# Shared and routed experts of a mixture layer as one sequence of 48 chunks

## Chip, cores, metric

One core of one Trainium2 chip. The time is the device time of one execution, in microseconds (us); of several runs the median counts. The kernel is an attention layer followed by a mixture-of-experts layer; the change touches the second.

## The reference

```python
# x: (8, 1024, 256) float32, after the attention layer; h = layernorm(x)
cap = 128                                  # int(1024 * 2.0 / 16)
scores = softmax(h @ gate_w.T).transpose(0, 2, 1)          # (8, 16, 1024)
topk_w, topk_idx = top_k(scores, cap)      # each expert takes 128 rows of each b
x_tok = take_along_axis(h[:, None], topk_idx[..., None], axis=2)
g = einsum('becd,efd->becf', x_tok, Wg)    # 16 experts, F = 512, D = 256
u = einsum('becd,efd->becf', x_tok, Wu)
eo = einsum('becf,edf->becd', gelu(g) * u, Wd) * topk_w[..., None]
flat = zeros((8 * 1024, 256)).at[flat_idx].add(eo)         # routed experts
shared = (gelu(h @ Ws_g.T) * (h @ Ws_u.T)) @ Ws_d.T        # shared expert, all rows
out = x + flat + shared
```

## The kernel before

The attention block comes first. It leaves in memory `out` (the layer's x), `xn2` (the normalised rows) and `xn2T` (the same, turned), and in SBUF `gate_scores`.

Then `feed_forward` (L931) runs twice, each time as a block of its own, at whose end all engines meet. The first call (`shared=True`) is the shared expert over all 8192 rows, in 16 chunks of 512 tokens. It also makes the lists: the 128 pairs of a row group b and an expert lie on 128 partitions, each with its 1024 scores, and 16 rounds on VectorE take the eight largest (`select`, parts 0, 1 and 2: maximum, index of the maximum, replacement by -1). The second call is the routed part: 16 experts with 8 x 128 gathered rows each, two chunks of 512 an expert, 32 chunks.

Matmuls are done in three passes for precision (`three`, L61 to L63): each operand is split into a high part (cast to fp32r, ScalarE) and a low part (the difference, VectorE). One chunk is, on TensorE, four groups `up` (each the gate and the up product for 128 of the 512 columns F, 12 matmuls of 512 columns) and one `down` (48 matmuls of 256 columns); the down product belongs to the chunk before and stands between group 1 and group 2. In the routed part the tokens of the next chunk are turned by eight transposes ahead of it (`turn_tokens`, L1377). In the shared part the tokens come turned out of `xn2T`.

The other engines' work for a chunk: ScalarE does four GELUs (L1194), four casts `high` (L1198), the cast of the next chunk's tokens (L1187 or L1190); VectorE four products (L1261), four `low` (L1265), the low part of the next tokens (L1253), the result of the chunk before (L1281 in the shared part, four scalings L1286 in the routed one), and in the shared part one round of selection. The results of the shared part are stored by SyncE, with x added; those of the routed part are added into `out` by GpSimd's indirect DMAs (`scatter`, L1152), four a chunk, as the gathers (`gather`, L1130) are. Weights of the next expert are split inside the chunks; two sets of split weights take turns, the shared expert uses set 1.

The order is that of the program on each engine. TensorE's `up(n, f)` waits for the product of the group two before (the banks `gu` are two), `down` for all four low parts of its chunk, a chunk's start for the low part of its tokens. All loops go through `groups`: a first body, a hardware loop over the middle ones, and a last body. In the shared call a body is two chunks (one b), in the routed one four (two experts).

At the end of the first call VectorE ends the lists, TensorE turns them (L1443, L1444), VectorE copies them to `taken_scores` and `taken_rows` (L1365, L1366). GpSimd does nothing in the first call; in the second it starts with the gathers of the routed chunks 0 and 1.

## Time and profile before

| | us |
|---|---|
| median of 3 runs | 2351.36 |
| the three runs | 2350.05 to 2356.03 |
| the profiled execution's own time | 2354.57 |
| its span, first to last instruction | 2352.2 |
| busy, share of the span: TensorE | 2186.0, 93% |
| VectorE | 1848.3, 79% |
| ScalarE | 1557.9, 66% |
| GpSimd | 1051.3, 45% |

The profile's page gives busy time by engine, then the span in 40 slices of 58.8 us with the clock that TensorE was granted. The attention block takes slices 1 to 25, the shared part runs from about 1480 to 1755 us, the routed part from about 1757 to the end. In the page's slices TensorE's digit is 9 nearly throughout, and 7 in the slice in which the shared part ends. A matmul's duration in the profile is longer than its distance to the next one, since matmuls are pipelined; what a piece of work costs TensorE is read from start to start.

### The profile page before, as it was taken

The page shows a single profiled execution, that of the slowest core. Times are in us where ns is not written, and L with a number is a line of the kernel's source. Part 1 is how long each engine was busy: PE and PEld are TensorE (multiplying, and loading weights), DVE is VectorE, ACT ScalarE, POOL GpSimd, SP SyncE. Part 2 cuts the span into 40 slices and gives each one's busy share as a digit, 9 for nine tenths or more (in the row PEclk, how much of TensorE's full clock was granted, in tenths as well). Part 3 has the DMA queues.
Part 4 walks back from the last instruction along what each step waited for, and adds up shares of the span by engine and source line. Part 5 has one row for each costly group of instructions (what it writes and reads, how often), then busy time and mean ns, then how long its engine had stood idle before and what let it go on. Part 6 is the DMA issues. An engine that isn't in the chain of part 4 may idle for free. (4 is left out here: it accounts for less than half of the span.)

```text
span 2352.2 us, 42150 instructions
## 1 busy us (share of the span) xinstructions
PE 2186.0 (93%) x15502; PEld 1270.0 (54%) x15502; DVE 1848.3 (79%) x3103; ACT 1557.9 (66%) x3056; POOL 1051.3 (45%) x1561
## 2 busy tenths in 40 slices
PE   4899999999999999999999997899979999999996
PEld 3233333334333333343333224788868888888986
DVE  4899999999999999999999993566654555555553
ACT  2489999999998998998998895333323334334332
POOL 4442555564465456456451220000004666666664
PEclk8699999999999999999999998899999999999998
DMA  4002013112122122122122012432313444544543
GB/s 114 5 26 35 17 41 71 35 45 67 35 67 65 33 61 53 35 61 51 35 59 46 24 44 74 135 107 81 106 61 101 105 101 107 109 96 109 112 91 36
DMA packets 204835, 156.19 MB, mean 66 GB/s; under 512 B 110080, under 2 KB 185728, under 8 KB 204672
## 3 DMA queue, kind: packets, MB, share of 16 engines
q1 hardware_dynamic: 180096, 120.47, 18.3%
q0 software_dynamic: 24576, 33.57, 8.3%
q8 instruction: 100, 1.64, 0.3%
q14 instruction: 63, 0.52, 0.1%
HBM read 78.50 MB, written 50.33 MB: 55 GB/s over the span
## 5 line engine op out<-in xcount | busy, mean ns | idle before, releaser
L604 DVE TENSOR_REDUCE sb_MX<-ring 128x1 f32<-128x512 f32 x2048 | 1281.7, 683 | 65.6 <-PE ring L874 41.9
L718 ACT ACTIVATE sb_PR<-rot 128x512 f32<-128x512 f32 x2048 | 1118.3, 610 | 124.0 <-PE rot L885 108.7
L874 PE MATMUL ring<-sb_KT,sb_QT 32*128 32x512 bf16 x2048 | 503.7, 391 | 76.4 <-DVE sb_MX L604 63.0
L896 PE MATMUL pv<-sb_PR,sb_VA 128*32 128x512 f32 x4096 | 548.0, 607 | 2.6 <-ACT sb_OT L770 0.6
L874 PEld LDWEIGHTS ring<-sb_KT,sb_QT 32*128 32x128 bf16 x2048 | 122.0, 91 | 674.1 <-DVE sb_MX L604 620.6
L885 PE MATMUL rot<-sb_QT,sb_KT 32*128 32x512 bf16 x2048 | 405.7, 386 | 0.9
L1194 ACT ACTIVATE ex_GL<-ex_gu 128x512 f32<-128x512 f32 x128 | 76.5, 598 | 348.6 <-PE ex_gu L63 346.4
L1261 DVE TENSOR_TENSOR ex_HF<-ex_GL,ex_gu 128x512 f32<-128x512 f32 x128 | 87.5, 683 | 252.1 <-ACT ex_GL L1194 252.1
L1109 POOL TENSOR_TENSOR ex_pool_scratch<-identity 128x1 f32<-128x1 f32 x96 | 35.4, 369 | 461.4 <-POOLq L951 316.6
L1152 POOL DMA_INDIRECT out<-ex_YS,ex_rows_out x128 | 209.9, 1640 | 43.6 <-issue 43.1
L61 PE MATMUL ex_gu<-ex_XH,weights_high 128*128 128x512 f32 x512 | 201.0, 393 | 2.4 <-DVE ex_XL L1253 2.4
L62 PE MATMUL ex_gu<-ex_XL,weights_high 128*128 128x512 f32 x512 | 200.6, 392 | 0.0
L63 PE MATMUL ex_gu<-ex_XH,weights_low 128*128 128x512 f32 x512 | 200.3, 391 | 0.0
L61 PE MATMUL ex_y<-weights_high,ex_HH 128*128 128x256 f32 x512 | 147.4, 288 | 2.9 <-DVE ex_HL L1265 2.9
L896 PEld LDWEIGHTS pv<-sb_PR,sb_VA 128*32 128x32 f32 x4096 | 80.7, 108 | 123.6 <-issue 67.3
L1194 ACT ACTIVATE sh_GL<-sh_gu 128x512 f32<-128x512 f32 x64 | 38.2, 597 | 162.8 <-PE sh_gu L63 162.8
L62 PE MATMUL ex_y<-weights_low,ex_HH 128*128 128x256 f32 x512 | 144.8, 283 | 0.0
L63 PE MATMUL ex_y<-weights_high,ex_HL 128*128 128x256 f32 x512 | 144.8, 283 | 0.0
L1130 POOL DMA_INDIRECT ex_XG<-xn,ex_rows_in x128 | 126.0, 984 | 39.7 <-issue 39.1
L61 PE MATMUL rot<-sb_WH,sb_XH 128*128 128x256 f32 x384 | 129.8, 338 | 15.0 <-ACT sb_PR L718 6.0
L388 POOL CAST sb_QP<-sb_MX 128x16 bf16<-128x16 f32 x64 | 16.3, 254 | 242.8 <-DVE sb_MX L610 242.7
L1261 DVE TENSOR_TENSOR sh_HF<-sh_GL,sh_gu 128x512 f32<-128x512 f32 x64 | 43.7, 683 | 91.7 <-ACT sh_GL L1194 91.7
(170 smaller groups left out, 4108.3 us busy)
## 6 DMA issues: line engine op xcount, KB each, us to landing
sb_XA<-x SPq DMA_DIRECT2D x8, 1024.0 KB, 5.4
sb_XR<-x SPq DMA_DIRECT2D x8, 1024.0 KB, 5.3
out<-sb_XR SPq DMA_DIRECT2D x8, 1024.0 KB, 4.5
xn<-sb_XN SPq DMA_DIRECT2D x8, 1024.0 KB, 4.6
xn2T<-sb_XT SPq DMA_DIRECT2D x8, 1024.0 KB, 4.2
sh_XG<-xn2T SPq DMA_DIRECT2D x16, 512.0 KB, 5.4
sh_X<-out SPq DMA_DIRECT2D x16, 512.0 KB, 4.8
weights<-WgT SPq DMA_DIRECT2D x16, 512.0 KB, 4.2
```

The costliest lines, as they stand in the source:

```text
L61: nc.tensor.matmul(out, a_hi, b_hi, start=first, stop=False)
L62: nc.tensor.matmul(out, a_hi, b_lo, start=False, stop=False)
L63: return nc.tensor.matmul(out, a_lo, b_hi, start=False, stop=last)
L604: nc.vector.reduce_max(MX[:, unit % 2, half, j, qt % 4:qt % 4 + 1], ring[m % RING][:], AX.X).then_inc(ring_done, 1)
L718: out = nc.scalar.activation(PR[V % P_STEPS][:, j, :], R[:], ACT.Exp, scale=0.25)
L874: nc.tensor.matmul(ring[m % RING][:], QT[g][r, P * qt:P * qt + P], KT[g][r, 512 * half:512 * half + 512], start=True, stop=True, tile_posi ...
L885: nc.tensor.matmul(R[:], KT[g][r, P * kt:P * kt + P], QT[g][r, 512 * qh:512 * qh + 512], start=True, stop=True, tile_position=(r.start, 0) ...
L896: out = nc.tensor.matmul(pv_bank[head(j), :], VA[b % 2][:, kt, 4 * g + j, :], PR[V % P_STEPS][:, j, :], start=(kt == 0), stop=(kt == TT - 1))
L1130: nc.gpsimd.indirect_dma_start(out=XG[k % 2][:, t, :], out_offset=None, in_=d["xn2"], in_offset=bass.IndirectOffsetOnAxis(ap=rows_in[:, b: ...
L1152: nc.gpsimd.indirect_dma_start(out=d["out"], out_offset=bass.IndirectOffsetOnAxis(ap=rows_out[:, b:b + 1], axis=0), in_=YS[k % 2][:, t, :] ...
L1194: nc.scalar.activation(GL[f % 2][:], gu[f % 2][:, 0, 0:N], ACT.Gelu).then_inc(gelu_ready, 1)
L1261: nc.vector.tensor_tensor(HF[f % 2][:], GL[f % 2][:], gu[f % 2][:, 1, 0:N], ALU.mult).then_inc(hf_ready, 1)
```

## The change

The two calls become one block with one sequence of 48 chunks: 16 shared (0 to 15) and 32 routed (16 to 47). `Chunk` holds what differs between them, `following` and `before` give the neighbours, so that the last shared chunk turns the tokens of the first routed one and the first routed chunk holds the down product and the result of the last shared one. `turn_tokens`, the splits and the waits count through. The tiles of the two calls become one set; the turned shared tokens lie in the same buffers `XG` as the gathered ones, as a view `XT`.

The selection gets its own place: four groups of two chunks with three rounds (5 and 4 parts), then two groups with two rounds (3 and 3 parts), then none in the last four chunks. In a chunk up to two parts stand behind the first two products and `low` 0, the others at the chunk's end. The result of the chunk before, which stood behind `product` 2 and `low` 1, now stands ahead of `product` 2, in all chunks. The lists are finished behind chunk 11, turned ahead of chunk 14 and copied there; GpSimd's gathers wait for `lists_ready` only. The weights of expert 0 are split inside chunks 14 and 15. SyncE stores the last shared chunk, then loads the weights of expert 1.

The core of the diff (blank lines left out):

```diff
-def feed_forward(nc, d, ident, SC, WT, IX, W, WH, WL, shared_out, B, shared):
+def feed_forward(nc, d, ident, SC, B):
...
+    SHARED = RS * KS
     ROUNDS = CAP // 8
-    SHARED_STORES = 16 * B * HALVES // 2
-    tag = "sh_" if shared else "ex_"
+    THREES, TWOS = 4, 2
+    STORED = 16 * RS
+    ROWS = 16 * CT
...
+        XT = [x[:].rearrange("p t d -> p (t d)").rearrange("p (k n) -> p k n", k=KD) for x in XG]
...
+        def groups(engine, body, R, upto=None, since=0):
+            upto = R if upto is None else upto
+            if since == 0:
+                body(0, True, False)
+                since = 1
+            if min(upto, R - 1) > since:
+                with engine.Fori(since, min(upto, R - 1)) as r:
                     body(r, False, False)
-            if R > 1:
+            if upto == R:
...
+                self.n = KS * r + k if shared else SHARED + KE * r + k
+                self.nth = r if shared else 2 * r + k // 2
+                self.expert = None if shared else 2 * r + k // 2
+                self.q = 1 if shared else k // 2 % 2
+                self.turn = 0 if shared else self.expert + 1
+                self.x_in = shared_in[self.c] if shared else gathered[self.c]
+                self.x_count = (16 if shared else 16 * CT) * (self.nth + 1)
+                self.ys_before = self.n if shared else SHARED + CT * (self.n - SHARED)
...
+            groups(sp, shared_group, RS)
+            store(RS - 1, KS - 1)
+            def load_next(e):
+                sp.wait_ge(wl_ready, 3 * (turn_of(e) + 1))
+                load_weights(e + 1)
+            for c in range(2):
+                sp.wait_ge(gathered[c], ROWS)
+            load_next(0)
+            with sp.Fori(1, E - 1) as e:
+                load_next(e)
...
+                if known(ch.n, SHARED + 2):
+                    pool.wait_ge(xl_ready, ch.n - 1)
+                else:
+                    pool.wait_ge(turned_full, ch.n - SHARED - 1)
...
+            pool.wait_ge(lists_ready, 1)
             own = Tally(settled)
-            gather(0, 0, own)
-            gather(0, 1, own)
+            gather(Chunk(False, 0, 0), own)
+            gather(Chunk(False, 0, 1), own)
...
+            groups(act, lambda r, first, last: [chunk(Chunk(True, r, k), last) for k in range(KS)], RS)
+            groups(act, lambda r, first, last: [chunk(Chunk(False, r, k), last) for k in range(KE)], RE)
...
+            def chunk(ch, first, last, own=None, s=0, parts=range(0)):
+                def choose(n, more=False):
+                    for p in parts[n:] if more else parts[n:n + 1]:
+                        select(s + p // 3, p % 3, own)
+                after = following(ch, last)
+                past = before(ch, first)
+                coming = coming_expert(ch, last)
+                product(ch, 0)
+                product(ch, 1)
+                low(ch, 0)
+                choose(0)
+                choose(1)
+                if after:
+                    split_tokens(after)
+                if past:
+                    result(past)
+                product(ch, 2)
+                low(ch, 1)
+                product(ch, 3)
+                low(ch, 2)
+                if coming:
+                    split_weights(*coming, 0 if ch.k % 2 == 0 else 2)
+                if coming and ch.k % 2 == 1:
+                    take_scores(*coming)
+                low(ch, 3)
+                if coming and ch.k % 2 == 0:
+                    split_weights(*coming, 1)
+                choose(2, True)
+            split_weights(None, 1, 0)
+            split_weights(None, 1, 1)
+            split_tokens(Chunk(True, 0, 0))
+            split_weights(None, 1, 2)
+            dve.wait_ge(sct_full, 1)
+            nc.vector.tensor_copy(sct[:], y[0:BE].rearrange("p a n -> p (a n)")).then_inc(sct_ready, 1)
+            dve.wait_ge(sct_ready, 1)
+            def three_rounds(r, first, last):
+                own = Tally(own_sem, 9 * r)
+                chunk(Chunk(True, r, 0), first, last, own, 3 * r, range(0, 5))
+                chunk(Chunk(True, r, 1), False, last, own, 3 * r, range(5, 9))
+            def two_rounds(r, first, last):
+                s = 3 * THREES + 2 * (r - THREES)
+                own = Tally(own_sem, 3 * s)
+                chunk(Chunk(True, r, 0), False, last, own, s, range(0, 3))
+                chunk(Chunk(True, r, 1), False, last, own, s, range(3, 6))
...
+            assert 3 * THREES + 2 * TWOS == ROUNDS
+            groups(dve, three_rounds, RS, THREES)
+            groups(dve, two_rounds, RS, THREES + TWOS, THREES)
+            own = Tally(own_sem, 3 * ROUNDS)
+            own.wait(dve)
+            own.inc(nc.vector.tensor_copy(indf[:], inds[:]))
+            own.wait(dve)
+            dve.wait_ge(row0_in, 16)
+            nc.vector.tensor_scalar(indf[:], indf[:], row0[:], None, ALU.add).then_inc(sel_ready, 1)
+            groups(dve, shared_group, RS, RS - 1, THREES + TWOS)
+            dve.wait_ge(sel_full, 1)
+            own.inc(nc.vector.tensor_copy(taken_scores[:].rearrange("p b e -> p (b e)"), turned[:, 0, 0:BE]))
+            nc.vector.tensor_copy(taken_rows[:].rearrange("p b e -> p (b e)"), turned[:, 1, 0:BE]).then_inc(lists_ready, 1)
+            own.wait(dve)
+            shared_group(RS - 1, False, True)
+            groups(dve, group, RE)
+            result(Chunk(False, RE - 1, KE - 1))
...
-                    product(n, 0)
-                    product(n, 1)
-                    low(n, k, 0)
-                    if shared:
-                        select(TURNS * n, 0, own)
-                    if not final:
-                        split_tokens(r if k < K - 1 else r + 1, (k + 1) % K)
-                    product(n, 2)
-                    low(n, k, 1)
-                    if shared:
-                        select(TURNS * n, 1, own)
-                    if not (first and k == 0):
-                        result(r if k else r - 1, (k - 1) % K)
-                    product(n, 3)
-                    low(n, k, 2)
-                    if more:
-                        split_weights(e, q, 0 if k % HALVES == 0 else 2)
-                    if more and k % HALVES == 1:
-                        take_scores(e, q)
-                    low(n, k, 3)
-                    if more and k % HALVES == 0:
-                        split_weights(e, q, 1)
-                    if shared:
-                        select(TURNS * n, 2, own)
-                        for s in range(1, TURNS):
-                            for part in range(3):
...
+            def chunk(ch, first, last):
+                after = following(ch, last)
+                past = before(ch, first)
+                if ch.k % 2 == 0:
+                    need_weights(ch, 2)
+                pe.wait_ge(xl_ready, ch.n + 1)
+                up(ch, 0)
+                up(ch, 1)
+                if after and not after.shared:
+                    turn_tokens(after)
+                if past:
+                    down(past)
+                up(ch, 2)
+                up(ch, 3)
...
+            groups(pe, shared_group, RS, RS - 1)
+            pe.wait_ge(sel_ready, 1)
+            nc.tensor.transpose(turned[:, 0, 0:BE], vals[:], ident[0:BE, 0:BE])
+            nc.tensor.transpose(turned[:, 1, 0:BE], indf[:], ident[0:BE, 0:BE]).then_inc(sel_full, 1)
+            shared_group(RS - 1, False, True)
+            groups(pe, group, RE)
+            down(Chunk(False, RE - 1, KE - 1))
...
-        feed_forward(nc, d, ident, SC, WT, IX, W, WH, WL, shared_out, B, True)
-        feed_forward(nc, d, ident, SC, WT, IX, W, WH, WL, shared_out, B, False)
+        feed_forward(nc, d, ident, SC, B)
```

## Rows read from the trace of the kernel before

**Rows 1.** windows by stage; us, each engine's busy time (x instructions), granted clock, DMA share, GB/s

```profile
1479.90:1738.00 258.10, 258.07 (x1465) 228.06 (x1466) 169.14 (x276) 83.25 (x139) 0.00 (x0) 0.99 0.29 94
...
1770.00:2330.00 560.00, 557.38 (x3272) 493.96 (x3271) 301.06 (x471) 211.79 (x332) 339.50 (x364) 1.00 0.46 99
```

**Rows 2.** timeline of TensorE at the boundary; start, us, instruction, [idle before it <- releaser]

```profile
1743.23 0.39 PE L63 MATMUL sh_gu<-sh_XH,weights_low 128*128 128x512 f32 x1
...
1747.74 0.39 PE L61 MATMUL sh_y<-weights_high,sh_HH 128*128 128x256 f32 x1 [4.12 <-DVE sh_HL L1265]
...
1755.08 0.27 PE L1443 MATMUL sh_turned<-identity,sh_vals 128*128 128x128 f32 x1
...
1765.32 1.97 PE L1377 MATMUL ex_turned<-identity,ex_XG 128*128 128x128 f32 x8 [9.86 <-DMA ex_XG<-xn,ex_rows_in]
...
1769.66 0.79 PE L61 MATMUL ex_gu<-ex_XH,weights_high 128*128 128x512 f32 x1 [2.36 <-DVE ex_XL L1253]
```

**Rows 3.** chain that ended last; start us, us, what (routed chunks)

```profile
1778.16 0.87 PE ex_turned L1377 x8
...
1789.96 0.87 PE ex_turned L1377 x8
...
1807.51 0.87 PE ex_turned L1377 x8
...
2298.63 0.87 PE ex_turned L1377 x8
```

**Rows 4.** windows inside the boundary, columns as in Rows 1

```profile
1748.20:1755.50 7.30, 7.26 (x49) 7.02 (x47) 4.90 (x7) 1.61 (x2) 0.00 (x0) 0.77 0.01 3
...
1769.66:1775.20 5.54, 5.54 (x13) 4.37 (x14) 0.02 (x1) 0.02 (x1) 3.41 (x6) 0.50 0.68 224
```

**Rows 5.** timeline of TensorE, chunks 14 and 15

```profile
1721.33 0.40 PE L61 MATMUL sh_gu<-sh_XH,weights_high 128*128 128x512 f32 x1
...
1732.24 0.28 PE L61 MATMUL sh_y<-weights_high,sh_HH 128*128 128x256 f32 x1
...
1737.99 0.40 PE L61 MATMUL sh_gu<-sh_XH,weights_high 128*128 128x512 f32 x1
```

**Rows 6.** timeline of VectorE, chunk 14, and the last round's end

```profile
1713.98 1.21 DVE L1303 MATCH_REPLACE8 sh_sct<-sh_v,sh_sct 128x1024 f32<-128x1024 f32 x1
...
1715.10 0.68 DVE L1261 TENSOR_TENSOR sh_HF<-sh_GL,sh_gu 128x512 f32<-128x512 f32 x1
...
1717.69 1.22 DVE L1297 MAX8 sh_v<-sh_sct 128x8 f32<-128x1024 f32 x1
...
1718.83 1.21 DVE L1253 TENSOR_TENSOR sh_XL<-sh_XG,sh_XH 128x1024 fp32r<-128x1024 f32 x1
...
1724.98 0.69 DVE L1261 TENSOR_TENSOR sh_HF<-sh_GL,sh_gu 128x512 f32<-128x512 f32 x1 [4.94 <-ACT sh_GL L1194]
...
1747.75 1.21 DVE L1303 MATCH_REPLACE8 sh_sct<-sh_v,sh_sct 128x1024 f32<-128x1024 f32 x1
...
1748.99 0.23 DVE L1356 CAST sh_indf<-sh_inds 128x128 f32<-128x128 uint32 x1
```

**Rows 7.** GpSimd's timeline, and the gathered tokens' tile (landing)

```profile
1757.40 0.19 POOL L1109 TENSOR_TENSOR ex_pool_scratch<-identity 128x1 f32<-128x1 f32 x1 [316.56 <-POOLq L951]
...
1762.59 0.95 POOL L1130 DMA_INDIRECT ex_XG<-xn,ex_rows_in  x1 [0.30 <-issue]
...
DMA to landing us min/median/max: 2.6/2.8/5.6
```

**Rows 8.** DMA issues (KB, median us to landing); weights' tile; ScalarE's timeline

```profile
weights<-WgT SPq DMA_DIRECT2D x16, 512.0 KB, 4.2
...
weights<-WuT SPq DMA_DIRECT2D x16, 512.0 KB, 6.0
...
DMA to landing us min/median/max: 3.8/6.0/9.9
...
1820.64 1.05 ACT L1179 CAST weights_high<-weights 128x1024 fp32r<-128x1024 f32 x1
```

More of the change, by code:

```diff
@@ L989, in feed_forward @@
         wl_ready = sem("wl_ready")
[L990 removed]
+        shared_in = [sem(f"shared_in{c}") for c in range(2)]
+        gathered = [sem(f"gathered{c}") for c in range(2)]
         x1_in = [sem(f"x1_in{c}") for c in range(2)]
@@ new lines, in store, with shared_group @@
+            def store(r, k):
+                n = r * KS + k
+                sp.wait_ge(ys_ready, n + 1)
+                sp.dma_start(rows("out", n), YS[k % 2][:]).then_inc(shared_out[k % 2], 16)
+            load(0, 0)
+            load_weights(None)
+            sp.dma_start(row0[:], d["row0"][0:BE, :]).then_inc(row0_in, 16)
+            load(0, 1)
+            load_x1(0, 0)
+            sp.wait_ge(wl_ready, 3)
+            load_weights(0)
+            def shared_group(r, first, last):
+                for k in range(KS):
+                    if not last:
+                        load(r + 1, k)
+                    if not (first and k == 0):
+                        store(r if k else r - 1, (k - 1) % KS)
+                    if not (last and k == KS - 1):
+                        load_x1(r if k < KS - 1 else r + 1, (k + 1) % KS)
@@ L1351, in _ @@
-            groups(dve, group)
-            if shared:
-                assert TURNS * CHUNKS == ROUNDS
-                own = Tally(own_sem, 3 * ROUNDS)
-                own.wait(dve)
-                own.inc(nc.vector.tensor_copy(indf[:], inds[:]))
-                own.wait(dve)
-                dve.wait_ge(row0_in, 16)
-                nc.vector.tensor_scalar(indf[:], indf[:], row0[:], None, ALU.add).then_inc(sel_ready, 1)
-                for i in range(3):
-                    split_weights(0, 0, i)
@@ new lines, in _, with shared_group @@
+            for t in range(TT):
+                out = nc.tensor.transpose(y[0:BE, t // 4, P * (t % 4):P * (t % 4) + P], SC[:, t, :], ident[:])
+            out.then_inc(sct_full, 1)
+            def shared_group(r, first, last):
+                for k in range(KS):
+                    chunk(Chunk(True, r, k), first and k == 0, last)
+            def group(r, first, last):
+                for k in range(KE):
+                    chunk(Chunk(False, r, k), first and k == 0, last)
+            groups(pe, shared_group, RS, RS - 1)
```

489 lines of the change are left out of this document (198 added, 291 removed).

## The prediction

> **What bounds the kernel now.** I read the windows by stage first, then the stretch between the shared and the routed part on TensorE, then the chain that ended last, and last the other engines around the chunks. In the shared part TensorE is busy for the whole stretch at a granted clock of 0.99, with VectorE at 169 us of 258 [rows 1]; in the routed part it is busy 557.4 of 560 us at 1.00 [rows 1]. Both parts are thus bound by TensorE's own matmuls, and no faster other engine would help. Between them they are not. The last matmul of chunk 15's gate and up products starts at 1743.23; then TensorE stands still 4.12 us for the last low parts of H, runs the down product, turns the two lists at 1755.08, stands still 9.86 us for the first gathered tokens, turns them, stands still 2.36 us for their high and low parts, and only at 1769.66 starts the routed chunk 0 [rows 2]. The halts also cost clock: the granted clock is 0.77 over the down product and 0.50, which is 1.2 of 2.4 GHz, over the first routed matmuls [rows 4]. The chain of waits shows that behind this every routed chunk is TensorE's work alone: one turn of tokens follows the other at 17.55 us (1789.96 to 1807.51), up to the last at 2298.63 [rows 3].
>
> **What a chunk costs TensorE.** Three rows of one kind of place give it: the third product group of chunk 14 starts at 1721.33, the down product inside chunk 15 at 1732.24, its third group at 1737.99 [rows 5]. So a shared chunk takes 16.66 us, a down product 5.75, and two of the four groups (16.66 - 5.75) / 2 = 5.45. A routed chunk has a turn of tokens besides: 0.87 in the chain [rows 3], and 16.66 + 0.87 = 17.53 is what the chain shows. A chunk starts with its first group; chunk 15's start is 1732.24 - 5.45 = 1726.79, chunk 14's 1710.13. Times written +x below are counted from a chunk's start.
>
> **The boundary (removed).** The change lets chunk 16 (the first routed one) start behind the last group of chunk 15, puts down(15) inside it, the turn of chunk 16's tokens inside chunk 15 and the turn of the lists ahead of chunk 14. I compare the same piece of TensorE's work before and after, from the last up matmul of chunk 15 to the turn of the tokens of the third routed chunk. Before: 1743.23 to 1789.96 = 46.73 us [rows 2, 3]. After, at full clock and without a halt: the last matmul's pitch 0.23, the two list transposes 0.22 (eight of that size are the 0.87 of a turn), one turn 0.87, two groups 5.45, and then the ordinary distance from turn to turn 17.55: 24.32 us. The difference is 22.4 us. It can be split to check it: halts 4.12 + 9.86 + 2.36 = 16.3; the slow clock: the down product 1747.74 to 1755.08 is 7.34 in place of 5.75 (1.6), the first turn 1.97 in place of 0.87 (1.1), the first two groups 1769.66 to 1778.16 are 8.50 in place of 5.45 (3.05); the rest, 0.3, are the drains of a last matmul ahead of a halt. Sum 22.35. The block's barrier lies inside the 9.86 and goes with it.
>
> **The selection (moved).** Before, each of the 16 shared chunks had one round (maximum, index, replacement). Now chunks 0 to 7 have 5 and 4 parts by turns, 8 to 11 three, 12 to 15 none. A part costs 1.14 us (the maximum at 1717.69, the next instruction at 1718.83) to 1.27 (the replacement at 1713.98, whose copy starts 0.15 earlier, the next product at 1715.10) [rows 6]. Three in a row, each waiting on the one before, is not in the trace; the nearest is the cast that waits for the last replacement: the replacement started at 1747.75 and took 1.21, and the cast starts 0.03 behind its end, at 1748.99 [rows 6]. So I take 1.3 a part and 1.4 as the upper end. VectorE is busy 169.1 us in 258 [rows 1], 11 us a chunk; without its round about 7.1, with 5 parts 13.6, with 4 parts 12.3, under 16.66 each. Its total stays the same.
>
> Where the order bites: behind a chunk with three parts at its end the next chunk's products start late. In the new order the fourth product no longer stands behind the result of the chunk before, so the lows end near +2.9; three parts take 4.0: product 0 at +6.9 in place of +4.97 (1715.10). TensorE needs it for its third group at +11.2: 4.3 spare. Product 1 +7.5 (needed at +13.9), low 0 +8.8 behind ScalarE's cast, two parts to +11.4, the tokens' low part to +12.5 (needed at +16.66: 4.2 spare), the result of the last chunk to +13.6. Product 2 waits for its GELU until +14.85 anyway (1724.98) and must be done by +16.66: it ends at +15.5. So VectorE has 1.2 us before product 2 is late and 1.2 more before TensorE is: 2.4 us is the least margin. The cost is 0, and what hides it is TensorE's 16.66 us; with the cover gone it is what exceeds 2.4 us, once in each of the 12 chunks.
>
> **The result ahead of product 2 (moved).** VectorE waits for y at about +11.4 (shared) or +12.3 (routed), with product 2, its low part and product 3 queued behind it; product 2 has its GELU only at +14.85 (+15.7 in a routed chunk), and four scalings take 1.6. Cost 0. ScalarE's casts hang on product 2 and 3, which don't move. The scatter is released some 3 us earlier, and nobody waits for it but the next scatter. At the very end product 3 stood 0.1 us behind the result; that is gained at most, and I leave it out.
>
> **Lists, gathers, weights (moved).** The lists are turned ahead of chunk 14. TensorE waits there for a cast done two chunks before: 0. VectorE waits for the transposes at +0.3 of chunk 14 while its lows of chunk 13 run to +2.9: 0; two copies (0.3 each) follow, ahead of product 0. GpSimd, which stood still 316.6 us until 1757.40, starts its gathers near +3.6 of chunk 14. Before, the fourth gather was issued at 1762.59, 5.2 us behind 1757.40, and a gather lands 2.8 us behind its issue [rows 7]: here +11.6. The turn is at 16.66 + 5.45 = +22.1 of the same count: 10.5 us spare. The next four wait for the low parts of chunk 15's tokens (about +9.5 of chunk 14), are landed by +18, and are needed one chunk later than that. The splitting of expert 0's weights (3 casts, 3 subtractions of 1.2) moves out of the halt into chunks 14 and 15, which have no selection: 7.1 + 2.4 + the four spare us, no cost. On SyncE the loading of expert 1's weights now stands behind the last shared store, which waits for the result of chunk 15 at +13.4 of chunk 16. Store 0.4, first load issued at +13.9, landed 4.2 later at +18.1, the second 0.5 and 6.0 later at +20.4 [rows 8]. ScalarE takes them at 1820.64 in the trace, +18.6 of that chunk, and 1.5 later at +20.1 [rows 8]. The first just makes it, the second is 0.3 late in front of a GELU whose product has over 5 us. Cost 0; both ends of this one: 0 to 3 us (rival 2).
>
> **The sum.** Span 2352.2 - 22.4 = 2329.8 us. The profiled execution took 2354.57, 2.4 over its span, so 2332.2 with the profile. That execution lies 3.2 above the median of the three runs, 2351.36; the gain has no reason to hang on that, so 2351.36 - 22.4 = 2329.0.
>
> **Rivals.** (1) VectorE stalls at the edges of its loops. It now has three short loops and two straight pieces where it had one loop. The trace of before speaks against a price: the replacement at 1713.98 is the last of the loop and the product at 1715.10 the first behind it, at the distance of 1.12 that the instruction's own time gives [rows 6]. If an edge cost a DMA's landing, 2.6 to 5.6 us [rows 7], TensorE would lose that less the margin of 2.4, 0.2 to 3.2 us, at five edges among the chunks with selection: 1 to 16 us, 2330 to 2345, typically 2335. The Trainium skill, page "Runtime: NRT & Kernel Launch", section "Instruction fetch mechanics", has a rule for it: a taken branch to a target outside the two pages held stops the engine until the page is fetched. By that rule this rival would happen; the row at 1715.10 shows no such stop at a loop's exit.
>
> (2) Late weights. With a landing of 9.9, the longest of these loads [rows 8], in place of 4.2, the first weights come at +23.8, 5.2 us behind ScalarE's turn; low 3 then ends that much later than its +21.3 and down(16) wants it at +23.9: TensorE stands 2.6 us, once. 2331.6 us.
>
> (3) Slower than before: the parts cost far more when they stand in a row with a wait ahead of each. Chunks 0 to 7 then take 7.1 + 4.5 parts on average and VectorE becomes the bound. Even with before is at 16.66 + 22.4 / 8 = 19.46 us a chunk, which is 2.75 us a part; at 3.0 it is 20.6 us, 31.5 us over eight chunks, 2360. For it: no row shows three in a row. Against it: 1.14 to 1.27 with other work behind, and 0.03 us between a replacement and an instruction that waits for it.
>
> (4) The change does not do what it says: the first gathers still come late, say because GpSimd is released only behind the last chunk. Then the halts of 9.86 and 2.36 and the slow first groups and turn (4.2) stay, and the gain is 6 us: 2345.
>
> **How the numbers follow.** Forecast 0.80; rival 1 0.08 (0.06 of it still faster), rival 2 0.05, rival 3 0.04, rival 4 0.03. A measurement of this kernel can tell about 0.3%, 7 us, from no change: faster is below 2344.3. Faster 0.80 + 0.06 + 0.05 = 0.91; same 0.02 + 0.03 = 0.05; slower 0.04. The range: the runs of before lie from 1.3 below to 4.7 above their median; below I add 2.7 for a boundary that costs still less than its full-clock sum, 2325. Above, 2329 + 4.7 + 2.6 for rival 2 and the lower part of rival 1 reach 2338.
>
> **What would show it.** In the profile of the changed kernel: no idle time of TensorE ahead of a routed matmul but the one ahead of the last down product, granted clock 1.0 from the first shared chunk to the end, 17.5 us from turn to turn beginning with the one inside chunk 15, 16.7 us a shared chunk also where three rounds stand. Product 0 of the chunks behind three parts starts near +6.9; gathers start about 30 us ahead of chunk 16; expert 1's weights are issued near +13.9 of chunk 16. Idle time of TensorE at the third group or at the first group of chunks 1 to 8, waiting for VectorE, would make the selection's step wrong; a TensorE that runs at 1.2 GHz somewhere behind 1490 would do so for the boundary's.

## The result, and the profile after

The changed kernel takes 2329.43 us (median of 4 runs, 2329.09 to 2331.80); the kernel before, beside it, 2350.70 (4 runs, 2348.56 to 2356.03). The ratio is 0.9903, with a 95% interval of 0.989 to 0.9917. The forecast was 2329.0, between 2325 and 2338. The profiled execution took 2329.34 us, with a span of 2327.6.

The windows by stage come first, as in [rows 1]: the stretch, its length, each engine's busy time (x instructions), granted clock, DMA share, GB/s. The first line is the start of the feed-forward part, the third runs from chunk 1 into chunk 13 and holds nearly all of the selection, the fourth chunks 14 and 15 with the lists and the gathers, the fifth the place where the boundary was, the last one lies in the last down product.

```profile
1475.60:1488.50 12.90, 12.80 (x48) 10.26 (x48) 7.54 (x11) 4.50 (x7) 0.00 (x0) 0.85 0.58 206
1488.50:1500.00 11.50, 10.56 (x67) 9.54 (x67) 11.17 (x22) 4.61 (x7) 0.00 (x0) 1.00 0.14 46
1500.00:1700.00 200.00, 200.00 (x1155) 177.26 (x1154) 144.69 (x234) 66.63 (x108) 0.00 (x0) 1.00 0.29 95
1700.00:1746.00 46.00, 46.00 (x258) 40.20 (x257) 24.28 (x33) 16.92 (x27) 14.72 (x19) 1.00 0.30 92
1746.00:1770.00 24.00, 24.00 (x160) 21.96 (x159) 12.39 (x15) 9.27 (x14) 4.37 (x7) 1.00 0.34 110
...
2305.40:2311.70 6.30, 6.20 (x40) 6.00 (x38) 0.06 (x1) 0.00 (x0) 0.29 (x1) 0.73 0.21 25
```

TensorE is busy without a gap from 1500 to 1770, at full clock, where it had stood still for 16.3 us and run at 0.77 and 0.50 [rows 2, 4]. All that it waits for from 1480 on is two instructions (the view of waits on TensorE: what waited, for what, us in total, times, longest):

```profile
PE ff_y L61 <- DVE ff_HL L1293: 2.9, 1, 2.9
PE ff_gu L61 <- DVE ff_HF L1289: 0.9, 1, 0.9
```

The first is the halt ahead of the last down product, which the kernel before has too. The second was not foreseen; it is told of below. The chain that ended last (start, us, what) now has the even step of 17.5 us from the turn of chunk 16's tokens on, which stands inside the shared part:

```profile
1728.75 0.87 PE ff_turned L1415 x8
1746.29 0.87 PE ff_turned L1415 x8
1763.84 0.87 PE ff_turned L1415 x8
```

Three rows of timelines show the order of the work: GpSimd's first instruction and its first gather, and the first list transpose ahead of chunk 14 on TensorE (start, us, instruction, idle before it and its releaser).

```profile
1709.67 0.20 POOL L1144 TENSOR_TENSOR ff_pool_scratch<-identity 128x1 f32<-128x1 f32 x1 [269.90 <-DVE ff_taken_rows L1398]
...
1710.85 1.24 POOL L1167 DMA_INDIRECT ff_XG<-xn,ff_rows_in  x1 [0.58 <-issue]
```

```profile
1706.22 0.27 PE L1478 MATMUL ff_turned<-identity,ff_vals 128*128 128x128 f32 x1
```

**Where the time went.** I compare one stretch in all kernels: from the first product of the feed-forward on TensorE to the turn of the tokens of the third routed chunk. Before it is 1479.93 to 1789.96, 310.03 us; after, 1475.69 to 1763.84, 288.15 us. The difference is 21.9 us, and the medians differ by 21.3. The spans differ by more, 24.6 us, because the stretch starts 4.24 us earlier in this execution and what follows it is 1.5 us longer. Neither comes from the change; the last section shows what they are.

The stretch itself begins with a piece that differs from one execution to the next: the first two groups of chunk 0, 24 matmuls, start at the lower clock, and the clock rises after 5.6 us in the execution before (matmuls of 0.63 us become ones of 0.40), after 3.6 in that after and after 4.8 in the repetition. So I also give the stretch without these 24 matmuls, from the third group of chunk 0 on. The rows of that group in before, after and the repetition:

```profile
1488.06 0.39 PE L61 MATMUL sh_gu<-sh_XH,weights_high 128*128 128x512 f32 x1
```

```profile
1483.00 0.39 PE L61 MATMUL ff_gu<-ff_XH,ff_WH 128*128 128x512 f32 x1
```

```profile
1484.61 0.39 PE L61 MATMUL ff_gu<-ff_XH,ff_WH 128*128 128x512 f32 x1
```

From there to the third routed turn it is 301.90 us before, 280.84 after and 280.83 in the repetition. The change is worth 21.1 us in this measure; the other 0.8 of the 21.9 is the clock at the start.

### The profile page after: what moved, and what is told of

Same layout as the page of the kernel before. It is cut to its first block and busy times, and to the rows that moved or that the text cites. A ratio compares the mean times of both kernels' runs of the same rounds, so it can differ in the third digit from the quotient of the medians.

```text
span 2327.6 us, 42123 instructions
## 1 busy us (share of the span) xinstructions
PE 2177.5 (94%) x15502; PEld 1263.6 (54%) x15502; DVE 1858.8 (80%) x3103; ACT 1560.0 (67%) x3056; POOL 1060.1 (46%) x1561
## 5 line engine op out<-in xcount | busy, mean ns | idle before, releaser
L61 PE MATMUL ff_gu<-ff_XH,ff_WH 128*128 128x512 f32 x768 | 300.4, 391 | 9.7 <-DVE ff_XL L1281 8.8
L62 PE MATMUL ff_gu<-ff_XL,ff_WH 128*128 128x512 f32 x768 | 300.1, 391 | 0.0
L63 PE MATMUL ff_gu<-ff_XH,ff_WL 128*128 128x512 f32 x768 | 299.6, 390 | 0.0
L1184 POOL DMA_INDIRECT out<-ff_YS,ff_rows_out x128 | 213.3, 1666 | 43.9 <-issue 43.5
L61 PE MATMUL ff_y<-ff_WH,ff_HH 128*128 128x256 f32 x768 | 220.6, 287 | 2.9 <-DVE ff_HL L1293 2.9
L62 PE MATMUL ff_y<-ff_WL,ff_HH 128*128 128x256 f32 x768 | 218.0, 284 | 0.0
L63 PE MATMUL ff_y<-ff_WH,ff_HL 128*128 128x256 f32 x768 | 218.0, 284 | 0.0
L61 PEld LDWEIGHTS ff_y<-ff_WH,ff_HH 128*128 128x128 f32 x768 | 147.9, 193 | 3.9 <-DVE ff_HL L1293 3.3
L62 PEld LDWEIGHTS ff_y<-ff_WL,ff_HH 128*128 128x128 f32 x768 | 148.0, 193 | 0.6
L63 PEld LDWEIGHTS ff_y<-ff_WH,ff_HL 128*128 128x128 f32 x768 | 148.0, 193 | 0.0
```

What stands on the lines that cost most here:

```text
L61: nc.tensor.matmul(out, a_hi, b_hi, start=first, stop=False)
L62: nc.tensor.matmul(out, a_hi, b_lo, start=False, stop=False)
L63: return nc.tensor.matmul(out, a_lo, b_hi, start=False, stop=last)
L1184: nc.gpsimd.indirect_dma_start(out=d["out"], out_offset=bass.IndirectOffsetOnAxis(ap=rows_out[:, b:b + 1], axis=0), in_=YS[ch.c][:, t, :], ...
```

## The experiments

Each run has the kernel before beside it on its chip. The ratio stands with its 95% interval; the stretch is the one defined above, read in the profiled execution. All of them in one table, in us, split at the third group of chunk 0; where two kernels are compared by the trace, the last column is the one to use.

| kernel | stretch | first two groups | from the third group |
|---|---|---|---|
| before | 310.03 | 8.13 | 301.90 |
| changed | 288.15 | 7.31 | 280.84 |
| changed, again | 288.67 | 7.84 | 280.83 |
| boundary back, gathers early | 298.86 | 7.23 | 291.63 |
| boundary back, gathers late | 310.69 | 8.41 | 302.28 |
| order of the selection alone | 309.83 | 8.03 | 301.80 |
| clock, 36 matmuls | 305.58 | 6.88 | 298.70 |
| clock, 27 matmuls | 304.12 | 7.33 | 296.79 |
| one more maximum | 291.74 | 8.15 | 283.59 |
| three more maxima | 296.46 | 6.96 | 289.50 |
| first chunk and end | 286.81 | 7.18 | 279.63 |
| first chunk alone | 286.91 | 7.28 | 279.63 |

### The changed kernel once more

> The changed kernel as it is, beside the next three on the same chip. Theory and rivals alike: 2329.4.

Measured: 2329.41 us, 0.9905 (0.9887 to 0.9924); the stretch is 288.67, half a microsecond from the first time, and that half lies in the first two groups. The result repeats, on the median as in the stretch.

### The boundary put back, the gathers early

```diff
-                return Chunk(False, 0, 0) if last else Chunk(True, ch.r + 1, 0)
+                return None if last else Chunk(True, ch.r + 1, 0)
...
             shared_group(RS - 1, False, True)
+            down(Chunk(True, RS - 1, KS - 1))
+            turn_tokens(Chunk(False, 0, 0))
             groups(pe, group, RE)
```

The first routed chunk likewise loses its chunk before (`before`), and VectorE and ScalarE get the like: the result of chunk 15, then the splitting of chunk 16's tokens, and only then the routed groups.

> The changed kernel, in one block, but the last shared chunk and the first routed one don't interlock: TensorE runs down(15) behind the last group of chunk 15, then turns the tokens of chunk 16, then starts chunk 16; VectorE and ScalarE in the same order. The gathers start as early as in the changed kernel. Theory (the gain is TensorE's halts and lost clock at the boundary, and half of it is the gathers): the halt for the lows of H is 2.9 us (no selection is in their way there), the halt for the first tokens' high and low parts 2.4 us, no halt for gathers, clock loss between 0 and 4.7 us: 5.5 to 10.5 us over the changed kernel, 2335 to 2340, most likely 2337. Rival (the gain is the new order of VectorE's work and the packed selection): no difference from the changed kernel, 2329.

Measured: 2340.22 us, 0.9948 (0.9931 to 0.9964). The boundary alone costs 10.8 us from the third group on, and the median moves by 10.8, a little past the 10.5 that was the upper end. TensorE's timeline has the two halts and no third; the turn of the tokens follows the down product at once, since the tokens landed long before:

```profile
1744.07 0.58 PE L61 MATMUL ff_y<-ff_WH,ff_HH 128*128 128x256 f32 x1 [4.08 <-DVE ff_HL L1294]
...
1752.09 1.04 PE L1418 MATMUL ff_turned<-identity,ff_XG 128*128 128x128 f32 x8
...
1755.53 0.50 PE L61 MATMUL ff_gu<-ff_XH,ff_WH 128*128 128x512 f32 x1 [2.41 <-issue]
```

Halts of 4.08 and 2.41 are 6.5 of the 10.8. The granted clock was 0.67 over the down product (1744.07 to 1751.5) and 0.62 over the first routed matmuls (1755.5 to 1760), 1.00 from 1760 on; I put the other 4.3 down to this and to the drains ahead of the halts, without having measured them apart. I had expected a first halt of 2.9. It is 4.08 because a subtraction of expert 0's weights, 1.2 us, stands ahead of the last low part of H on VectorE:

```profile
1742.12 1.22 DVE L1269 TENSOR_TENSOR ff_WL<-ff_W,ff_WH 128x1024 fp32r<-128x1024 f32 x1
```

The kernel of the next section but one, which has no such subtraction there, has a halt of 2.85.

### The boundary put back, the gathers late

The kernel above, and GpSimd waits for the last shared result ahead of its first gather:

```diff
             pool.wait_ge(lists_ready, 1)
+            pool.wait_ge(ys_ready, SHARED)
```

> As the kernel with the boundary undone, and besides GpSimd starts the first gathers only behind the result of chunk 15. Theory: 9.9 us of waiting for gathers come back, with all of the clock loss (5.7 us in all): 3.0 + 9.9 + 2.4 + 5.7 = 21 us over the changed kernel, 2350, as the kernel before, some 13 us over the kernel with early gathers. Rival (the gain is VectorE's order and packing): 2329. Rival (the block's own end and start cost several us): clearly less than the kernel before, 2345.

Measured: 2351.28 us (10 runs), 0.9999 (0.999 to 1.0009); stretch 310.69.

```profile
1767.22 1.97 PE L1419 MATMUL ff_turned<-identity,ff_XG 128*128 128x128 f32 x8 [9.39 <-DMA ff_XG<-xn,ff_rows_in]
```

The late tokens cost 9.39 us of halt, and the turn behind them runs at half clock, 1.97 in place of 0.87. The median is 11.1 above the kernel with early gathers and 0.1 us from the kernel before beside it. The gain thus has two parts of like size: 10.8 us for the routed chunk that starts without a pause, and 10.7 from the third group on for the early gathers (11.8 in the stretch, of which 1.2 is the slow start). One block in place of two does not bring the gain: this kernel has the one block and the selection's new order and takes the time of the old one. What the barrier costs by itself this run doesn't tell, since I chose what releases the late gathers. They wait for the result of chunk 15, and GpSimd starts 8.7 us behind the start of the down product; before, behind the lists and the barrier, it was 9.7.

### The selection's order alone

The kernel before, with the new packing of the selection and the result ahead of product 2:

```diff
-                    if shared:
-                        select(TURNS * n, 0, own)
+                    for p in part[0:2]:
+                        select(s + p // 3, p % 3, own)
...
-                    product(n, 2)
-                    low(n, k, 1)
-                    if shared:
-                        select(TURNS * n, 1, own)
                     if not (first and k == 0):
                         result(r if k else r - 1, (k - 1) % K)
+                    product(n, 2)
+                    low(n, k, 1)
                     product(n, 3)
```

> The kernel before with its two blocks and its boundary, and with VectorE's new order and the selection packed into the first 12 shared chunks (5 and 4 parts, then 3 and 3). Theory: the packing and the order cost and gain nothing while TensorE is the bound, but for 0.9 us of TensorE waiting in the first chunk, as seen in the changed kernel, and 1.2 us gained because no selection delays the last lows of H: within 0.5 us of the kernel before, 2350. Rival (they bring the gain): 2329 to 2335. Rival (they cost and the boundary brings more than 22 us): 2355.

Measured: 2351.95 us (10 runs, 2349.96 to 2356.62), 0.9995 (0.9985 to 1.0005); stretch 309.83. The new order by itself neither costs nor brings anything in the time. It has one halt of 0.9 us that the kernel before doesn't have, behind chunk 0, and its first halt at the boundary is 2.85 where it was 4.12; the two nearly cancel. Its use is only that the selection is over by chunk 11, so that the lists can be turned ahead of chunk 14.

### The clock alone

What does the lower clock at the boundary cost? The kernel before gets matmuls of no use in its halts, whose results nobody reads: 16 ahead of the last shared down product, a number of them ahead of the first turn of tokens and 10 behind it. The outputs don't change.

```diff
             groups(pe, group)
+            if shared:
+                idle_work(16)
             down(R - 1, K - 1)
...
             if not shared:
+                for _ in range(WARM):
+                    nc.tensor.matmul(gu[0][:, 0, 0:N], WH[0][0][:, 0, 0:P], WH[0][1][:, 0, :], start=True, stop=True)
                 turn_tokens(0, 0)
```

> The kernel before with matmuls of no use put into TensorE's three halts at the boundary (16 ahead of down(15), 36 ahead of the first turn of tokens, 10 behind it), so that the halts stay and the clock does not fall. Theory: the slow clock is a share of its own of the gain, 1.6 + 1.1 + 3.05 = 5.75 us: 2345. It could be less by 1 to 2 us where the added matmuls end behind the data. Rival (the halts alone count, the first routed groups being held by other engines): 2351, no difference.

Measured with WARM = 36: 2348.88 us (10 runs), 0.9982 (0.9973 to 0.9992); 3.2 us less than before from the third group on. The 36 ended about 2 us behind the landing of the tokens, so they ate a part of what they saved:

```profile
1755.70 10.05 PE L1420 MATMUL ex_gu<-weights_high 128*128 128x512 f32 x36 [1.95 <-PEq L952]
```

They took 10.05 us at a granted clock of 0.83; at 0.23 from start to start, the full-clock step, 36 of them would take 8.3 (an estimate) and end 0.3 us behind the landing. So most of the 2 us is the clock, which was down for a part of the 36 though TensorE was at work. I tried again with 27:

> The kernel before with matmuls of no use in TensorE's three halts, now 27 in place of 36 ahead of the first turn of tokens, because the 36 ended about 2 us behind the landing of the tokens. From the first matmul of the shared part to the turn of the third routed chunk's tokens the kernel before takes 310.0 us, the one with 36 305.6. Theory (slow clock 5.75 us in all; what the down product gains runs on through the gathers): 304.3, 5.7 less than before, and the median 2351 less 5.7: 2345.5. Rival (keeping the clock gains only at the first routed groups, 3 us): 307, 2348.

Measured: 2346.81 us (10 runs, 2344.2 to 2352.6), 0.9983 (0.9972 to 0.9994) of the runs beside it (median 2350.68).

```profile
1748.86 6.40 PE L1420 MATMUL ex_gu<-weights_high 128*128 128x512 f32 x27 [1.95 <-PEq L952]
...
1756.84 1.09 PE L1378 MATMUL ex_turned<-identity,ex_XG 128*128 128x128 f32 x8 [1.57 <-DMA ex_XG<-xn,ex_rows_in]
```

```profile
1745.00:1752.00 7.00, 5.05 (x31) 4.29 (x30) 2.49 (x4) 0.00 (x0) 2.22 (x5) 1.00 0.24 78
1757.00:1765.00 8.00, 7.95 (x39) 6.38 (x39) 1.99 (x3) 1.61 (x2) 4.71 (x8) 1.00 0.44 134
1765.00:1775.00 10.00, 10.00 (x50) 8.38 (x49) 5.62 (x8) 5.73 (x10) 6.56 (x10) 1.00 0.63 209
```

The 27 took 6.40 us, the full-clock step, behind the same halt of 1.95. The tokens still come at their time, and every window from 1735 to 1775 is at clock 1.00. The stretch is 5.9 less than before, but 0.8 of that lies in the first two groups; from the third group on it is 5.1. That is the clock's share of the boundary in the trace, where 5.75 was foreseen. The median moved by 3.9, between the two expectations; with runs of one kernel spread over 8 us it doesn't decide between them, and the trace is nearer to the first. Useless work in the halts can thus win about a quarter of what the change wins in the trace, 3.9 of 21.3 us on the median.

### How much room VectorE has

The margin of 2.4 us is the one number on which the selection's cost of nothing hangs. So VectorE gets more to do at the worst place: one, or three, further maxima over a 128 x 1024 tile of zeros behind the first two products of each of the 12 chunks with selection. Their results aren't used, and the outputs don't change.

```diff
                 choose(1)
+                for x in range(3 if parts else 0):
+                    nc.vector.max(spare8[:, 8 * x:8 * x + 8], spare[:])
```

> The changed kernel with one more maximum (1.25 us, over a tile of zeros, of no use) on VectorE in each of the 12 chunks with selection, ahead of the tokens' low part. Theory (VectorE's work is covered, the least margin is 2.2 to 2.4 us a chunk): nothing in 11 chunks, 1.25 us in the first one, where TensorE already waits 0.9 us for product 2: 2330.7. Rival (no margin, each operation lies on the path): 12 x 1.25 = 15 us, 2344.

Measured: 2336.05 us, 0.9928 (0.9907 to 0.995); stretch 291.74.

```profile
1495.62 0.76 PE L61 MATMUL ff_gu<-ff_XH,ff_WH 128*128 128x512 f32 x1 [2.06 <-DVE ff_HF L1292]
```

Behind eleven of the twelve chunks there is no halt, as the margin says. From the third group on the kernel is 2.8 us longer, and all of it comes behind chunk 0: a halt of 0.94 became 2.06, and behind it the clock was at 1.2 GHz (0.51 over 1495.6 to 1499.1), with a matmul of 0.76 in place of 0.47. The median is 6.6 over the changed kernel, where 1.3 was expected, and more than the trace shows. In the profiled execution the feed-forward also starts late, at 1479.81, where the two of the changed kernel have 1475.69 and 1476.77; other executions, of kernels without this edit, have it between 1473.68 and 1481.09, so these 4 runs can't tell how much of the 6.6 that is, and the rest of it stays open.

> As before with three more maxima a chunk, 3.75 us. Theory: past the margin of 2.2 to 2.4 us in the chunks behind three parts: 1.3 to 1.5 us in each of 4 odd chunks, nothing to 0.5 in the others, 3.75 in the first: 7 to 12 us, most likely 9: 2338.5. Rival (no margin): 12 x 3.75 = 45 us, 2374. Rival (a margin of over 4 us): 3.75 us, 2333.

Measured: 2341.69 us (5 runs), 0.9957 (0.9940 to 0.9973). The median is 12.3 over the changed kernel, just past the 7 to 12 expected, and from the third group on it is 8.7. The waits for the product are 7.0 us in four places:

```profile
PE ff_gu L61 <- DVE ff_HF L1292: 7.0, 4, 4.3
```

```profile
1497.57 0.77 PE L61 MATMUL ff_gu<-ff_XH,ff_WH 128*128 128x512 f32 x1 [4.32 <-DVE ff_HF L1292]
...
1550.28 0.50 PE L61 MATMUL ff_gu<-ff_XH,ff_WH 128*128 128x512 f32 x1 [0.89 <-DVE ff_HF L1292]
...
1584.82 0.50 PE L61 MATMUL ff_gu<-ff_XH,ff_WH 128*128 128x512 f32 x1 [0.84 <-DVE ff_HF L1292]
...
1619.36 0.50 PE L61 MATMUL ff_gu<-ff_XH,ff_WH 128*128 128x512 f32 x1 [0.91 <-DVE ff_HF L1292]
```

The last three lie 34.5 us apart, two chunks each: they stand at the first group of chunks 4, 6 and 8 and wait for product 2 of chunks 3, 5 and 7, which come behind three parts. Three further maxima of 1.13 us are 3.4 us, and 0.9 of them is seen: the margin is 2.5 us, where the prediction had 2.4. Chunk 1 also comes behind three parts and shows no halt; TensorE had just been held back 4.3 us there.

### Two edits more: the first chunk, and the end

The new stall behind chunk 0 has a plain remedy. That chunk has no down product of a chunk before it, so TensorE wants its product 2, at the first group of chunk 1, 5.75 us earlier than in any other; its index search can wait until behind the products. And the last down product can be given to its readers in quarters, each scaled and scattered while the next is computed, with the banks of the turned tokens, free by then, for the first two.

```diff
                 choose(0)
-                choose(1)
+                if past:
+                    choose(1)
...
-                choose(2, True)
+                choose(2 if past else 1, True)
...
+                        place = (turned, turned, y, y)[t][:, t % 2, 0:D] if end else y[:, t // 2, D * (t % 2):D * (t % 2) + D]
...
+                    if end or t == CT - 1:
+                        out.then_inc(y_full, 1)
```

> The changed kernel with two edits: in the first chunk only one part stands in the middle and four at its end, so that TensorE does not wait 0.9 us for product 2; and the last down product is cut into four quarters of 128 tokens in four banks, each with its own signal, so that its scaling and its scatter start behind the first quarter. Theory: the end is a chain of down product, four scalings and four scatters at 1.86 us each; with quarters the scatters run beside the down product and the end comes 5.3 us earlier (6.7 where the clock falls in the last down product), with the first chunk's 0.9: 6.2 to 7.6 us, 2322.5. Rival (the end is set by the landing of the scatters' data or by the block's end, not by their issue): only 0.9 us, 2328.5.

Measured: 2322.29 us (2320.75 to 2326.15), 0.9878 (0.9858 to 0.9899). It beats both kernels, the changed one by 7.1 us. From the third group on it takes 1.2 us less than the changed kernel, and the waits of TensorE have one line left, the 2.9 ahead of the last down product. On VectorE each quarter is scaled in 0.48 us as soon as it is there, and GpSimd's four scatters follow one another 1.86 us apart, the first beside the down product:

```profile
2304.24 0.48 DVE L1318 TENSOR_SCALAR ff_YS<-ff_turned,ff_WC 128x256 f32<-128x256 f32 x1 [1.78 <-PE ff_turned L63]
2305.68 0.48 DVE L1318 TENSOR_SCALAR ff_YS<-ff_turned,ff_WC 128x256 f32<-128x256 f32 x1 [0.96 <-PE ff_turned L63]
```

```profile
2305.15 1.56 POOL L1186 DMA_INDIRECT out<-ff_YS,ff_rows_out  x1 [0.15 <-issue]
...
2310.73 1.55 POOL L1186 DMA_INDIRECT out<-ff_YS,ff_rows_out  x1 [0.30 <-issue]
```

From the last turn to the last scatter's issue it is 39.8 us, where the two executions of the changed kernel have 46.8 (2272.49 to 2319.30) and 45.3.

> The changed kernel with only the first chunk's selection moved (one part in the middle, four at the end); the end as in the changed kernel. Theory: 0.9 us of waiting and up to 0.5 of clock behind it go, 2328.2, and from the first shared matmul to the turn of the third routed chunk's tokens 286.8 us as in the kernel with both edits, 288.2 to 288.7 in the changed one. Rival (the end's quarters brought all): 288.4 and 2329.4.

Measured, with the first of the two edits alone: 2332.60 us (2330.12 to 2334.82), 0.9926 (0.9909 to 0.9943). From the third group on it is again 1.2 us less than the changed kernel, 279.63 as in the kernel with both edits, and no wait for the product is left. That is what was expected, but the median is 3.2 above the changed kernel's, not below. In its profiled execution the last down product is slow (42.4 us from the last turn to the first scatter, for 41.2 and 39.7). That needs no edit: the kernel before with the 27 matmuls and the changed one with three more maxima show 42.4 as well. The intervals of 0.9926 and 0.9905 overlap. That the first edit is worth anything on the median is therefore not shown; only the two together are.

## Why the prediction was right

**The boundary.** The step carries the whole forecast. Foreseen were 24.3 us from the last up matmul of chunk 15 to the third routed turn. In the trace that matmul starts at 1740.46 and the turn at 1763.84, 23.4 us; with the list transposes and one turn, which now lie ahead of it, 24.5. From the third group of chunk 0 on, before and the kernel with the first chunk mended, which lacks the stall told of below, are 22.3 us apart (301.90 and 279.63), against the 22.4 foreseen. The runs split the gain in two ways. By cause, the lower clock is 5.1 us against the 5.75 of the sum; the rest is halts. By edit, 10.8 is the pause and 10.7 the late gathers. These two go from the changed kernel back to one that stands within 0.4 us of before from the third group on. The selection's order alone makes 0.1 there, which fits the nothing that the prediction gave it; that the barrier costs nothing beyond what the wait for the gathers hides was argued and isn't shown by itself.

**The selection.** A part was taken at 1.3 us. Three in a row start at 1525.91, 1527.16 and 1528.69 on VectorE, steps of 1.25 and 1.53, and the product behind them at 1529.83, 1.14 later. That product is product 0 of chunk 3, at +6.95 by the even step of 16.66 us; foreseen was +6.9. Product 2 of that chunk waits for its GELU until +14.84 (foreseen +14.85), with VectorE idle for 1.05 us ahead of it, where the prediction had 1.2:

```profile
1525.91 1.21 DVE L1327 MATCH_REPLACE8 ff_sct<-ff_v,ff_sct 128x1024 f32<-128x1024 f32 x1
1527.16 1.22 DVE L1321 MAX8 ff_v<-ff_sct 128x8 f32<-128x1024 f32 x1
...
1528.69 1.22 DVE L1324 FIND_INDEX8 ff_i<-ff_v,ff_sct 128x8 uint32<-128x1024 f32 x1
1529.83 1.27 DVE L1289 TENSOR_TENSOR ff_HF<-ff_GL,ff_gu 128x512 f32<-128x512 f32 x2
...
1537.72 0.69 DVE L1289 TENSOR_TENSOR ff_HF<-ff_GL,ff_gu 128x512 f32<-128x512 f32 x1 [1.05 <-ACT ff_GL L1228]
```

The step of 1.53 holds a wait of 0.16 and the copy between the maximum and the index search; the bound of 1.4 was a little low, the value of 1.3 right for the sum of the three.

**What it missed.** The margin was worked out for a chunk behind three parts. Chunk 0 is another case: with no down product in it, TensorE is through with its last two groups 5.75 us earlier, and there the maximum, the index search and the tokens' low part stand ahead of product 2. The halt, at the first group of chunk 1, is 0.94 us and costs 1.2, as the kernel with the first chunk mended shows:

```profile
1489.54 0.47 PE L61 MATMUL ff_gu<-ff_XH,ff_WH 128*128 128x512 f32 x1 [0.94 <-DVE ff_HF L1289]
```

Idle time at the first group of chunks 1 to 8, waiting for VectorE, was a sign that the prediction named for its selection's step being wrong. By this sign the step, whose cost was put at 0, failed for chunk 0 and held for the eleven others. It is also the place that breaks first when VectorE gets more work, before the margin of the other chunks is used up. Nor was the clock 1.0 throughout: 0.85 in the first window, and 0.73 in the window of the last down product, behind 1490 but far from the boundary.

**Lists, gathers, weights.** GpSimd starts at 1709.67, +3.3 of chunk 14 (foreseen +3.6); the fourth gather goes out at 1715.24, and landing 2.8 later it is there at +11.7 (foreseen +11.6), 10.7 us ahead of the turn at 1728.75. The first load of expert 1's weights is issued at 1754.71, +14.0 of chunk 16 (+13.9), and ScalarE takes it at 1759.67, +19.0 (+18.6). VectorE waits 0.34 us for it, TensorE not at all. So rival 2, late weights, and rival 4, late gathers, fell with the trace of after.

**The other rivals.** Rival 3, parts of 2.75 us, fell with the rows above. Rival 1, stalls at the edges of VectorE's loops, was to show at five places as idle time of TensorE or as distance between VectorE's instructions. TensorE is busy 200.00 of 200.00 us from 1500 to 1700. And on VectorE the replacement that is the last instruction of a loop's round and the product that is the first of the next are 1.13 us apart, where the loop goes round (1544.06 to 1545.19) as where it is left (1610.70 to 1611.83), the distance of two instructions in a row:

```profile
1544.06 1.21 DVE L1327 MATCH_REPLACE8 ff_sct<-ff_v,ff_sct 128x1024 f32<-128x1024 f32 x1
1545.19 1.38 DVE L1289 TENSOR_TENSOR ff_HF<-ff_GL,ff_gu 128x512 f32<-128x512 f32 x2
...
1610.70 1.21 DVE L1327 MATCH_REPLACE8 ff_sct<-ff_v,ff_sct 128x1024 f32<-128x1024 f32 x1
1611.83 1.38 DVE L1289 TENSOR_TENSOR ff_HF<-ff_GL,ff_gu 128x512 f32<-128x512 f32 x2
```

The Trainium skill, page "Runtime: NRT & Kernel Launch", section "Instruction fetch mechanics", lets a taken branch outside the two pages held stop an engine until its page is fetched. No stop shows at these edges. Whether their targets lie outside the two pages no run here shows, so the prediction's "by that rule this rival would happen" took more from the rule than it says, and the trace doesn't test the rule.

**The sum and the range.** The median lies 0.4 us over the forecast, and that this is so little is partly luck. The medians differ by 21.3 us, 1.1 less than the 22.4 foreseen, which is about the missed 1.2; and the forecast started from 2351.36, 0.7 over the median of the runs beside, which hides most of it.

## What to carry to other kernels

A boundary between two parts that are each bound by one engine costs three things at once: the drain of the pipeline, what the next part waits for, and the clock that TensorE loses in between; the whole is read in one distance, from a row ahead of the boundary to the first row of the even step behind it. Both the pause and the late transfers have to go: here early transfers alone left half of the cost, and joining the two blocks with both put back left all of it. When an engine's order is repacked to free a later place, work out the margin for the first and the last chunk too, where a piece of the work that gives the margin is missing.

## What the runs showed of the hardware that was not expected

**TensorE's clock comes out differently from one execution to the next, in fixed places.** The first place is the logits, ahead of the feed-forward, in code that the change doesn't touch. Their 32 matmuls take 6.85 us in the profiled execution of before and 3.73 in that of after (TensorE's timelines, one row of each):

```profile
1459.89 6.85 PE L857 MATMUL rot<-sb_gw,sb_XT 128*128 128x16 f32 x32
```

```profile
1458.82 3.73 PE L857 MATMUL rot<-sb_gw,sb_XT 128*128 128x16 f32 x32
```

The granted clock is 0.50 over 1455 to 1467 of before, 0.70 over 1450.8 to 1462.8 of after. That is 3.1 of the 4.24 us by which the stretch starts earlier; the other 1.1 is attention, which ended that much sooner. The same kernel shows both values: in the repetition of the changed kernel the 32 matmuls take 6.85 us again. The second place is the start of the feed-forward, where the clock rises 3.6 us behind the first matmul in one execution of the changed kernel and 4.8 in the other. The third is the last down product. Before it ran at 1.00; in after the clock is 0.73 for a part of it, as the last window above shows, and from the last turn to the first scatter it is 41.2 us, in the repetition 39.7 at a clock of 1.00, and 39.8 before. Together such places are 3 to 5 us of a span with no instruction changed, of the size by which single runs of one kernel lie apart (25 runs of before: 2349.08 to 2356.53). The Trainium skill, page "TensorE: Matmul & The Clock Gate", section "Part 1: The HAM clock gate", tells of one kernel with different counts of slow matmuls at its start from run to run. These traces show the like further on, at the start of a stage and at the kernel's last product. For a change of less than 5 us, a stretch of the trace that leaves these places out is a better measure than a few runs: the two executions of the changed kernel differ by 0.01 us in it.

**The length of a halt alone doesn't say whether the clock falls behind it.** Behind the halt of 0.94 us ahead of chunk 1 the window is at 1.00; behind one of 2.06 in the same place the first matmul takes 0.76 for 0.47, and 1.1 us more of halt made the kernel 2.8 longer. But behind the halt of 1.95 us ahead of the useless matmuls the clock stayed up in one run (27 in 6.40 us) and was down for a part in the other (0.66 over 1755.7 to 1759.2). And the halt of 2.9 us ahead of the last down product is followed by a first matmul of 0.39 and 0.38 us in the two executions of the changed kernel, and of 0.58 in five of the other kernels.
